# Queries and keys of the first two tiles of a banded attention made one stage earlier, part of the band mask moved from TensorE to VectorE, and fewer split steps on GpSimd

## The reference, cut to what matters

```python
# 1: linear attention with decay, 16 query heads, 4 key/value heads of 128, chunks of 64
x = layernorm(x + lightning(x, wq, wk, wv, wo))
# 2: attention over the channels: for each of 32 items the 256 channels are the
#    sequence, the 64 rows its features, 8 heads of width 8
q, k, v = split(x_item.T @ w_in.T + b_in)
scores = q k^T / sqrt(8)
scores = where(|i - j| <= 64, scores, finfo.min)      # the band
o = softmax(scores) @ v
y = relu(o @ w_out.T + b_out) * encodings
x = layernorm(x + y @ w_ct + b_ct)
```

## Time and profile before

| | |
|---|---|
| median of three runs | 3537.84 us (3532.89 to 3541.11) |
| the profiled execution | 3529.02 us |
| its span, first to last instruction | 3527.3 us |
| PE busy | 3259.2 us, 92% of the span |
| first stage | 0 to 379 us |
| banded stage | 379 to 691 us |
| granted clock of PE, mean | 0.965 |

### The profile page before, as it was taken

How to read it: one execution, slowest core, us unless ns; L and a number is a source line. 1 busy time by engine, 2 the same in 40 slices (tenths; PEclk the granted TensorE clock), 3 DMA queues, 4 the chain that set the end, 5 groups by cost and what they waited for, 6 DMA issues and landing times. The chain is left out here.

```text
span 3527.3 us, 95956 instructions
## 1 busy us (share of the span) xinstructions
PE 3259.2 (92%) x37316; PEld 2275.0 (64%) x37316; DVE 2351.7 (67%) x4366; ACT 1945.2 (55%) x5229; POOL 2083.7 (59%) x3086
## 2 busy tenths in 40 slices
PE   9999699897899999999999999999998688689996
PEld 6777466565577777777777777777776355356665
DVE  5555266534687888777787878788777588444443
ACT  1111155422576677666777677666775377545555
POOL 3333388643566666666666666666666267657774
PEclk9999699998999999999999999999999799899998
DMA  2000455100211111111111111111111456366655
GB/s 85 13 13 7 117 124 126 47 1 4 73 53 52 51 51 50 51 47 47 49 54 52 45 56 51 52 43 52 48 40 33 92 152 170 109 218 210 212 183 230
DMA packets 223129, 278.60 MB, mean 79 GB/s; under 512 B 58548, under 2 KB 186872, under 8 KB 216280
## 3 DMA queue, kind: packets, MB, share of 16 engines
q1 hardware_dynamic: 203340, 237.24, 23.6%
q0 software_dynamic: 18432, 34.96, 2.9%
q10 hardware_dynamic: 908, 0.27, 0.1%
HBM read 162.13 MB, written 125.83 MB: 82 GB/s over the span
## 5 line engine op out<-in xcount | busy, mean ns | idle before, releaser
L2215 PE MATMUL head_ring<-gd_xT,head_w 128*128 128x512 f32 x1024 | 507.8, 619 | 8.5 <-DMA head_w<-gd_w 5.4
L1547 POOL DMA_INDIRECT ytok<-exp_arena,exp_cur x256 | 251.1, 981 | 117.2 <-issue 72.1
L2543 DVE TENSOR_TENSOR head_Xs<-head_bx,head_join 128x512 bf16<-128x512 f32 x320 | 219.7, 686 | 81.7 <-PE head_bx L2257 81.7
L2215 PEld LDWEIGHTS head_ring<-gd_xT,head_w 128*128 128x128 f32 x1024 | 175.2, 191 | 147.4 <-issue 134.8
L2508 DVE SCALAR_TENSOR_TENSOR head_cb_V<-head_ring,head_taps,head_cb_V 128x504 f32<-128x504 f32 (+2 forms) x384 | 263.0, 726 | 2.8 <-ACT head_cb_V L2370 2.8
L2340 PE MATMUL head_by<-head_wo,head_ogT 128*128 128x256 f32 x1016 | 253.1, 392 | 7.1 <-ACT head_ogT L2450 0.4
L2224 PE MATMUL head_ring<-head_w,gd_xT 128*128 128x256 f32 x1024 | 257.4, 394 | 0.0
L2340 PEld LDWEIGHTS head_by<-head_wo,head_ogT 128*128 128x128 f32 x1016 | 182.5, 189 | 37.2 <-DVE rows_xc L2576 13.7
L2224 PEld LDWEIGHTS head_ring<-head_w,gd_xT 128*128 128x128 f32 x1024 | 185.3, 191 | 32.2 <-issue 0.3
L2415 ACT CAST head_Tt<-head_btt 128x512 bf16<-128x512 f32 x320 | 194.1, 607 | 17.8 <-PE head_btt L2265 16.0
L2435 ACT COPY head_U<-head_bu 128x512 f32<-128x512 f32 x256 | 137.4, 589 | 109.9 <-PE head_bu L2303 109.9
(11 more groups left out here) (366 smaller groups left out, 9293.1 us busy)
## 6 DMA issues: line engine op xcount, KB each, us to landing
xbuf<-head_blank SPq DMA_DIRECT2D x64, 552.0 KB
exp_arena<-xbuf SPq DMA_DIRECT2D x64, 552.0 KB, 5.3
head_gi<-scan SPq DMA_DIRECT2D x64, 256.0 KB, 4.8
ytok<-head_blank SPq DMA_DIRECT2D x64, 256.0 KB
exp_arena<-ytok SPq DMA_DIRECT2D x14, 1024.0 KB, 12.3
moe_w<-moe_w SPq DMA_DIRECT2D x32, 384.0 KB, 3.2
cb_Q<-qd SPq DMA_DIRECT2D x45, 192.0 KB
cb_K<-kd SPq DMA_DIRECT2D x45, 192.0 KB
```

Of the source, the lines that this page charges most:

```text
L1547: pool.indirect_dma_start(ytok, bass.IndirectOffsetOnAxis(ap=cur[i % AHEAD][s][:, b:b + 1], axis=0), y[i % RESULTS][s][:, b, :], None, bou ...
L2215: last = pe.matmul(b[:, :], w[:, c, FEAT[what]], xT[:, c, n % UNITS * N:n % UNITS * N + N], start=c == 0, stop=c == DC - 1)
L2543: dve.tensor_tensor((Ti if a == 0 else Xs)[:, :, :], bx[:, :].rearrange("p (q i) -> p q i", i=SEQ), join[:, a, :].unsqueeze(1).broadcast_t ...
```

## The change

Three things are done.

1. Tiles 0 and 1 of the banded stage are prepared in the last turn of the first stage. Behind slot 0's last output product PE makes q and k of both tiles from the rows that were stored in turn 0 and are loaded back (`first`). ACT adds the biases and makes the first bf16 parts, POOL the others in three steps, SP writes them to `qd` and `kd` and reads them back into their places. A class `Hold` keeps what outlives a stage: four places for Q and K of two tiles (they are where the first stage's weights `wqk` and its rotation tables were, and later hold `gi` and `ex` of the delta stage and Q and K of the second channel attention), the band, the identity and the query and key weights. A table `OPENING` says where the first occurrence of a step stands. The remaining weights are issued by ACT.
2. In the pairs 1, 4 and 6 of each eight (`SUMMED`) PE leaves the band matmul out, and DVE adds the band and takes the maximum with `tensor_tensor_reduce`, four times 192 elements. It writes the sums back to PSUM, where nobody reads them.
3. The first bf16 part is cast by ACT (a step "cast"), and the last rest is written as bf16 directly: three split steps on POOL in place of five, and four in place of five for the maxima. "turn" and "place" come one unit later, "ratio" one unit earlier.

```diff
+class Hold:
+    PLACE = 2 * D * 4
+    AHEAD = 2
...
@@ stage_lightning
+                store(TURNS - 1, 0)
+                for t in range(Hold.AHEAD):
+                    for i in range(3):
+                        if i:
+                            sp.wait_ge(split_step, t * 3 + i + 1)
+                        else:
+                            sp.wait_ge(cast_ready, t + 1)
+                        for half, scratch, copies in ((0, qd, (i,)), (1, kd, (i, i + 3) if i < 2 else (i,))):
+                            for row in copies:
+                                sp.dma_start(scratch[t, row * 8:row * 8 + 8, :].rearrange("d (j c) -> j d c", c=D),
+                                             part[t][:, i, half, :]).then_inc(spread_in[t], 16)
...
+                for t in range(Hold.AHEAD):
+                    sp.wait_ge(spread_in[t], 8 * 16)
+                    for i in range(3):
+                        rows = slice(i * 24, i * 24 + 24)
+                        sp.dma_start(hold.heads(2 * t)[rows, :, :].rearrange("p j c -> p (j c)"), qd[t, 0:24, :]).then_inc(gather_in, 16)
+                        sp.dma_start(hold.heads(2 * t + 1)[rows, :, :].rearrange("p j c -> p (j c)"), kd[t, i * 8:i * 8 + 24, :]).then_inc(gather_in, 16)
+                store(TURNS - 1, 1)
...
+                        if (turn, k, u) == (TURNS - 1, Y0, 0):
+                            pe.wait_ge(first_in, 5 * 16)
+                            for t in range(Hold.AHEAD):
+                                pe.matmul(bank_of[t][:, 0:D], xwq[:, :], first[:, t, :], start=True, stop=True)
+                                pe.matmul(bank_of[t][:, D:2 * D], xwk[:, :], first[:, t, :], start=True, stop=True).then_inc(twin_filled, 1)
...
@@ stage_banded
-    SLOTS, RING, GROUP, LAG, FIRSTS, BEHIND = 4, 12, 4, 32, 4, 6
+    SLOTS, RING, GROUP, LAG, BEHIND, AHEAD = 4, 12, 4, 32, 6, Hold.AHEAD
+    SUMMED = (1, 4, 6)
...
-    plan = {"prepare": -36, "split0": -35, "split1": -33, "split2": -31, "split3": -29, "split4": -27, "spread": -28, "gather": -17, "values": -2, "fetch": -8, "tops": 17, "turn": 21,
-            "place": 22, "unload": 53, "sort": 55, "invert": 56, "ratio": 58, "wo": 63, "ct": 66, "close": 67, "store": 70}
+    plan = {"prepare": -36, "cast": -35, "split0": -34, "split1": -32, "split2": -30, "spread": -28, "gather": -17, "values": -2, "fetch": -8, "tops": 17,
+            "turn": 22, "place": 23, "unload": 53, "sort": 55, "invert": 56, "ratio": 57, "wo": 63, "ct": 66, "close": 67, "store": 70}
+
+    OPENING = {"fetch": (0, -1), "prepare": (2, 8), "cast": (2, 9), "values": (0, 10), "split0": (2, 9), "split1": (2, 11), "split2": (2, 13),
+               "spread": (2, 14), "gather": (2, 19)}
...
-                        pe.matmul(b[:, 0:QB * KW], ident16[:, :], band16[:, :], start=True, stop=False, skip_group_check=True)
+                        plain = n % H // 2 in SUMMED
+                        if not plain:
+                            pe.matmul(b[:, 0:QB * KW], ident16[:, :], band16[:, :], start=True, stop=False, skip_group_check=True)
...
+                    elif what == "cast":
+                        act.wait_ge(qk_ready, n - AHEAD + 1)
+                        if n >= AHEAD + 2:
+                            act.wait_ge(spread_in[n % 2], (n - 2) // 2 * WRITES)
+                        act.copy(part[n % 2][:, 0, :, :], qk[n % 2][:, :, :]).then_inc(cast_ready, 1)
...
+                        if j // 2 in SUMMED:
+                            for a in range(2):
+                                for i in range(QB):
+                                    held = near[n // 2 % 2][:, a * 512 + i * KW:a * 512 + i * KW + KW]
+                                    last = dve.tensor_tensor_reduce(out=held, in0=held, in1=band[:, i * KW:i * KW + KW], scale=-1.0, scalar=3e38,
+                                                                    op0=ALU.add, op1=ALU.min, accum_out=top[t % 2][:, i, j + a:j + a + 1])
+                            last.then_inc(top_ready, 1)
+                        else:
...
-                        if step % 2 == 0:
-                            pool.tensor_copy(part[u][:, i, :, :], left[:, :, :]).then_inc(split_step, 1)
-                        else:
-                            pool.tensor_tensor(rest[u][:, :, :], left[:, :, :], part[u][:, i, :, :], ALU.subtract).then_inc(split_step, 1)
+                            pool.wait_ge(cast_ready, n - AHEAD + 1)
+                            pool.tensor_tensor(rest[u][:, :, :], qk[u][:, :, :], part[u][:, 0, :, :], ALU.subtract).then_inc(split_step, 1)
+                        elif step == 1:
+                            pool.tensor_copy(part[u][:, 1, :, :], rest[u][:, :, :]).then_inc(split_step, 1)
+                        else:
+                            pool.tensor_tensor(part[u][:, 2, :, :], rest[u][:, :, :], part[u][:, 1, :, :], ALU.subtract).then_inc(split_step, 1)
```

More of the change, by code:

```diff
@@ L133, in stage_lightning @@
         qk = [m.sb(f"qk{u}", [P, QK, N]) for u in U]
-        ra = [[m.sb(f"ra{u}{k}", [P, 512]) for k in range(2)] for u in U]
-        rb = [[m.sb(f"rb{u}{k}", [P, 512]) for k in range(2)] for u in U]
+        ra = [[late[:, 2 + k, :] for k in range(2)], [m.sb(f"ra1{k}", [P, 512]) for k in range(2)]]
+        rb = [[late[:, 4 + k, :] for k in range(2)], [m.sb(f"rb1{k}", [P, 512]) for k in range(2)]]
         v = [m.sb(f"v{u}", [P, TS, HKV * DH]) for u in U]
@@ L145, in stage_lightning @@
         bank = [[m.ps(f"bank{u}{k}") for k in range(4)] for u in U]
+        bank_of = [bank[0][(Y0 + 1 + t) % 4] for t in range(Hold.AHEAD)]
+        xwq, xwk, xbq, xbk, xbqs = hold.wq, hold.wk, hold.bq, hold.bk, hold.bqs
+        first = m.sb("first", [P, Hold.AHEAD, D])
+        twin = [qk[0][:, 2 * t:2 * t + 2, :] for t in range(Hold.AHEAD)]
+        part = [sT[0][:, t, 0:3 * D].bitcast(BF16).rearrange("p (c a k) -> p c a k", c=3, a=2) for t in range(Hold.AHEAD)]
+        SCALE = float(np.float32(1.0) / np.sqrt(np.float32(8)))
         BLOCK = 4
@@ L303, in _ @@
                                      b[:, :].rearrange("p (h n) -> p h n", h=2 * G)).then_inc(o_ready[u], 1)
+                        elif (turn, k, u) == (TURNS - 1, Y0, 0):
+                            act.wait_ge(first_in, 5 * 16)
+                            act.activation(xbqs[:, :], xbq[:, :], ACT.Copy, scale=SCALE).then_inc(scaled, 1)
+                            act.wait_ge(scaled, 1)
+                            for t in range(Hold.AHEAD):
+                                act.wait_ge(twin_filled, t + 1)
+                                act.activation(twin[t][:, 0, :], bank_of[t][:, 0:D], ACT.Identity, bias=xbqs[:, :], scale=SCALE)
+                                act.activation(twin[t][:, 1, :], bank_of[t][:, D:2 * D], ACT.Identity, bias=xbk[:, :]).then_inc(twin_ready, 1)
+                                act.wait_ge(twin_ready, t + 1)
+                                act.copy(part[t][:, 0, :, :], twin[t]).then_inc(cast_ready, 1)
             @block.vector
@@ L408, in timeline @@
             for what, offset in plan.items():
-                if (g - offset) % H == 0 and 0 <= (g - offset) // H < TILES:
-                    yield what, (g - offset) // H
+                n, shifted = (g - offset) // H, OPENING.get(what, (0, offset))
+                if (g - offset) % H == 0 and shifted[0] + (what in OPENING) <= n < TILES:
+                    yield what, n
+                if what in OPENING and g == shifted[1]:
+                    yield what, shifted[0]
     def since(n):
@@ L532, in _ @@
                             pe.wait_ge(*held)
-                        pe.matmul(misc[:, 0:T], w["xa_wq"][:, :], x[:, n, :], start=True, stop=True)
-                        pe.matmul(misc[:, T:2 * T], w["xa_wk"][:, :], x[:, n, :], start=True, stop=True).then_inc(qk_filled, 1)
-                        held = (qk_ready, since(n + 1))
+                        pe.matmul(misc[:, 0:T], hold.wq[:, :], x[:, n, :], start=True, stop=True)
+                        pe.matmul(misc[:, T:2 * T], hold.wk[:, :], x[:, n, :], start=True, stop=True).then_inc(qk_filled, 1)
+                        held = (qk_ready, n - AHEAD + 1)
                     elif what == "values":
@@ L626, in _ @@
             def _(act):
-                act.wait_ge(early_in, 16 * len(early))
-                act.activation(bq[:, :], bias["xa_bq"][:, :], ACT.Copy, scale=SCALE).then_inc(bq_ready, 1)
-                act.wait_ge(bq_ready, 1)
+                for t, name in loads:
+                    act.dma_start(t, A[name]).then_inc(weights_in, 16)
                 for what, n in timeline():
@@ L663, in _ @@
             def _(dve):
-                dve.wait_ge(weights_in, 16 * len(loads))
                 for what, n in timeline():
@@ L1274, in early_weights @@
                 lower(sp, i)
-        stage_cross(nc, xc, qd, kd, rows, xbuf, early_weights, A)
+        stage_cross(nc, xc, hold, qd, kd, rows, xbuf, early_weights, A)
         with ExitStack() as ctx:
```

203 lines of the change are left out of this document (111 added, 92 removed).

## The result

| | before | changed |
|---|---|---|
| median of the runs, us | 3535.4 (6 runs, 3532.89 to 3541.11) | 3510.19 (6 runs, 3504.28 to 3511.75) |
| profiled execution, its own time, us | 3529.02 | 3511.75 |
| its span, us; granted TensorE clock | 3527.3; 0.965 | 3510.0; 0.966 |

The ratio of the medians is 0.9929, 95% interval 0.9916 to 0.9942: faster by 25 us. The forecast was 3517.0 us, 20.8 less than the 3537.84 known then, with a range from 3503 to 3533. The table's "before" joins the three runs shown earlier with three made beside the changed kernel.

The account below looks back on a forecast made before the run. PE was taken to bound the kernel, busy 3259.2 of 3527.3 us, with POOL close behind in the banded tile. Start -23.9 and 14 steady tiles +3.1 gave -20.8 us, from 3537.84 to 3517.0 us; range 3503 to 3533.

Parts of the forecast that it names:

- C0: First output score of the banded stage, behind 32 units of near scores; forecast at 407.9 us instead of 431.8.
- the start: Opening of the banded stage: queries and keys of tiles 0 and 1 made earlier bring the first output score 23.9 us forward.
- 1.8 us on PE, which bounds that stage: First stage's last turn: four added f32 matmuls of 256 columns, 0.44 us each, lengthen it by 1.8 us.
- 8 us of cover: First stage's end: last read goes out at about 370, the store is due at 378.0, leaving 8 us.
- start gives less: Rival: late reads or a late tile 2 put the first output score at some 415, total 3524 us; 9%.
- The add-and-reduce: DVE's new instruction in summed pairs: 0.39 us each, between 0.33 and 0.55; a pair 1.56 us, +0.62.
- Prepare's wait: Unit 12 of a tile: PE waits 0.76 us for the misc bank, because ratio stands behind summed pair 4.
- Sort's wait: Turn one unit later, directly ahead of sort: PE waits 0.45 us a tile for ACT's copy of turn's result.
- GpSimd: 0 taken: Lighter POOL in the steady tile: at most 0.45 us a tile; nothing counted, 6 us kept for the range.
- The sum of a tile: Steady tile: -0.99 for the band matmuls, +0.76 and +0.45 for waits, +0.22 us; 14 tiles +3.1.
- the waits stay out: Rival: add-and-reduce costs 0.33 us, POOL's relief is felt, PE keeps nearly all 13.9 us; total 3500 us; 13%.
- DVE becomes the bound: Rival: add-and-reduce at half rate, 0.7 us each, a tile +2.5 us, 14 tiles +34, total 3548 us; 8%.

Follow-up runs that it names:

- e9: Changed kernel with the twelve reads of tiles 0 and 1 issued at the banded stage's start, not the first stage's end; 0.9915 of before, one run.
- e4: Changed kernel with summed pairs 1, 5 and 6 in place of 1, 4 and 6; 0.9941 of before, 15.95 us a tile.
- e8: Changed kernel with summed pairs 1, 5, 6 and turn and place back one unit earlier, at 21 and 22; 0.9968 of before, one run; 15.94 us a tile.
- e3: Changed kernel, mix kept, with GpSimd's old five split steps and five for the maxima, no cast on ACT; 0.9934 of before, 16.64 us a tile.
- e11: Changed kernel with summed pairs 1, 5, 6 and the third split step three units later (-27 for -30); 0.9917 of before, 15.45 us a tile.
- e2: Changed kernel with no summed pairs, all band matmuls back on PE, opening and lighter GpSimd kept; 0.9938 of before, 16.11 us a tile.
- e5: Changed kernel with the first stage's last store issued from ScalarE's queue; 0.9994 of before, one run; 16.35 us a tile.
- e10: The changed kernel itself, measured again beside a candidate; 0.9944 of before, 16.36 us a tile.
- e12: Changed kernel with summed pairs 1, 5, 6, third split three units later, turn and place back at 21 and 22; 0.9915 of before, 15.39 us a tile.
- e6: Changed kernel whose first stage's end doesn't wait for the twelve reads; PE waits for them in the banded stage; 0.9958 of before, one run.
- e7: Changed kernel with last store from ACT, reads not awaited, tile 0's reads behind the first third of tile 1's writes; 0.9975 of before, one run.

## Why the prediction was right, and where its steps were not

The time came out right and the shape too: a first near score that waits for no transfer of its own, C0 some 21 us earlier, a steady tile that gains nothing. In the banded stage's end the sum even falls on the microsecond (-20.76 against -20.8). That is luck in part, since terms were wrong in both directions: the start gave 2.7 us less than forecast, 14 tiles at -0.02 in place of +0.22 us gave 3.4 more, and 0.7 us stand in neither.

- **"1.8 us on PE, which bounds that stage": 0 in the two profiled executions.** The four pairs of records take 1.7 us (349.48 to about 351.2), but the last output product ends at 372.58, before at 372.69. PE stood idle 1.78 us before, waiting for DVE's la_sT, and after 0.84 there and 0.29 for la_oT. That covers 0.65 us. The rest is the clock (third number from the end): the 24 matmul records behind that wait took 4.5 us before, at 0.62, and 3.1 after, at 1.00. First before, then after:

```profile
354.13:358.61 4.48, 4.48 (x24) 3.38 (x25) 0.00 (x0) 2.13 (x4) 0.00 (x0) 0.62 0.10 34
```

```profile
349.00:358.50 9.50, 8.37 (x59) 5.63 (x58) 4.44 (x12) 5.94 (x12) 6.93 (x10) 1.00 0.22 62
```

If the clock had stayed up there before, part of the 1.8 us would presumably show; no other execution of before was profiled.

- **"8 us of cover": none.** I reckoned when the last read is issued (370, measured 370.99 with its own 0.36) and forgot what it carries. The step that failed is the store's cover, counted in issue time on the queue instead of in bytes: 2.36 MB were under way until 382, and the restart came 4.8 us late (7.4 against 2.6 in e9). This is the "start gives less" rival in its first half, at a smaller price; with the 1.8 us that weren't lost, the first near score came 2.5 us late (383.55 for 381.0) and C0 2.7 (410.59 for 407.9). From the one to the other it was 27.0 us, forecast 26.9: following SP's queue gave that. Inside, tile 2's prepare came 0.7 us later than taken, its first write 1.0 us sooner behind it, and C0 0.5 us later behind the place; the spreads, the landing and the reads took what was taken for them. (The sum in the prediction has a slip of 0.2 us: 381.0 + 4.4 is 385.4.)
- **The add-and-reduce: 0.39 us taken, 0.31 measured, below the lower bound of 0.33.** I had held that "nothing in the rows lets it cost less", with at least 0.06 for the read. A read is recorded with 0.14 us but starts together with the next main instruction and has no step of its own. The main instruction's 0.4 us record, too, overlaps the next by 0.08. A pair takes 1.20 to 1.24 us; by the drain rule of the Trainium skill (VectorE: DVE Perf Modes, The DRAIN you can't avoid) alone the prediction's estimate was 2.2, and the trace doesn't bear that out here.
- **Prepare's wait: 0.76 taken, 0.45 measured** (4.5 us in ten waits). The place and the instruction are the ones named. With pair 4 at 1.20 instead of 1.56 us the same working gives 0.33 + 0.17 - 0.10 = 0.40, so nearly the whole miss is the term above. e4 took the wait down to 0.20.
- **Sort's wait: 0.45 taken, 0.10 measured**, and e8 shows that it was worth nothing in the tile.
- **GpSimd: 0 taken; -0.29 us a tile shown by e3.** I kept it for the range. But PE's wait for the banding *grew*, from 3.9 to 6.4 us in nine tiles, because the cheaper and earlier PE arrives at V sooner and the third split stands in the way (e11 moves it and the wait goes). So relief and new wait are in one row, and only e3, with 9.1, takes them apart.
- **The sum of a tile:** -0.99 + 0.45 + 0.10 + 0.28 (V) = -0.16, measured -0.02, forecast +0.22. The terms that the waits show leave 0.14 us unexplained, and in e4 they promise 0.6 where 0.4 came. I haven't settled it. (The tile of before is 16.37 us, not 16.40: the 605.8 of the earlier trace rows is the second record of a prepare that starts at 605.50.)

The rival "the waits stay out" was false for the changed table and nearly true for e11's, whose tile is 0.9 us shorter than before: 12.9 us for 14 tiles, near the 13.9 that the mix could give. But 0.26 us of each tile are GpSimd's (16.37 to 16.11, e2); 0.66 us a tile, 9.2 us, lie between e2 and e11. "DVE becomes the bound" fell with the first pair: a step of 0.31 us where it decides from 0.6, and DVE is busy 61.4 of 80 us. The Trainium skill (Vector Engine (DVE) Microarchitecture Reference, Points that are easy to get wrong) gives a half rate for an S2S2D2_STT instruction with two non-bf16 sources in SBUF. The trace calls this one CUSTOM_DVE_ANT_0 and doesn't say whether it is of that shape. With one of its two sources in PSUM no half rate shows: at half rate, twice the 1.02 ns an element of the earlier trace rows, 192 elements alone would take 0.39 us, and the step is 0.31.

The medians differ by 25.2 us, the stage by 20.8 in the profiled executions. The difference isn't in any row: the profiled execution of before was 6.4 us under its median, that of after 1.6 above. The clock, below, can move a single execution by nearly as much. Of the signs that I had named as mine of being wrong none came (a tile of 17.5 us, 10 us of waiting for cb_top, the store behind 379), but of those of being right the first near score (380 to 382) and the step of the add-and-reduce (0.35 to 0.45) missed.

## What to carry to other kernels

Moving reads to the end of an earlier stage hides their latency, not their bytes (4.8 us here): count the bytes that are in flight when the stage's last store is issued, since a barrier waits for both. An operation moved from a bound engine to one with room pays only where the bound engine doesn't wait in order for what stands behind it; the same edit cost 0.24 us a tile in one slot and, one pair and one split later, gave 0.66 beside e2, whose split stood where the change puts it. Two edits made at once can cancel to no change: undo each before both are called useless.

## What the chip showed that I had not expected

Behind C0 the granted TensorE clock drops to 1.2 GHz in some executions and stays at 2.4 GHz in others. Busy times by stretch of the changed kernel, then of e5, which differs from it by one store's queue:

```profile
411.00:426.00 15.00, 15.00 (x94) 10.58 (x96) 7.46 (x25) 7.77 (x18) 6.56 (x13) 0.50 0.57 134
```

```profile
411.00:426.00 15.00, 14.54 (x157) 10.31 (x157) 11.37 (x40) 11.11 (x25) 12.57 (x27) 1.00 0.72 168
```

At half the clock 94 matmul records stand in 15 us, at the full one 157. From C0 to the next stage it is 259.5 us (260.1 in e10) against 254.5 in e5, which has the same tile: the fall costs 5 us; between e4 and e8 (255.6 and 249.5, again one tile) it is 6. What stood before it is a wait of PE for transfers, just ahead of its densest stretch. PE's waits in the last us before C0, of the changed kernel, of e12 (which fell) and of e5 (which didn't):

```profile
408.60 0.34 PE L646 MATMUL cb_near<-hold_band,hold_ident 128*128 128x384 bf16 x1 [0.57 <-DMA cb_K<-kd]
```

```profile
414.00 0.33 PE L671 MATMUL cb_score<-hold_place 75*128 75x192 bf16 x2 [1.97 <-DMA hold_place<-cb_topT]
```

```profile
411.27 0.33 PE L672 MATMUL cb_score<-hold_place 75*128 75x192 bf16 x2 [0.53 <-DMA hold_place<-cb_topT]
```

The changed kernel waited 0.57 us there and then the 1.49 at C0 shown with the result. Over all thirteen executions with the new start and the one of before, the six in which the clock fell at or behind C0 (changed, e4, e10, e11, e12, before) waited 1.4 to 3.1 us for transfers in the last 3 us before it, the others at most 0.6, save e8: 1.42 us and no fall, where e10 waited 1.37 and fell. So some 2 us of waiting go with 5 more behind them, and the line between is thin. It isn't shown that the wait is the cause. In e3, e6 and e7 the clock had fallen already, more than 12 us earlier; of e3:

```profile
399.00:408.00 9.00, 8.17 (x39) 4.95 (x38) 7.18 (x21) 0.37 (x1) 3.32 (x8) 0.50 0.81 166
```

There PE came to C0 0.6 to 1.8 us later than in the changed kernel and had no transfer to wait for. Counted from the first near score to the next stage, e6 and e7 take 283.8 and 283.7 us, e5 281.8, the changed kernel 286.5: they had paid a part ahead of C0. Of the executions with the new start only the changed kernel's, e4's and e10's show no low clock between 396 and 408. e12 was to settle whether the earlier turn keeps the clock up. It doesn't: where it expected a clock near 1.00, from 411 to 426, the clock was 0.65, and at C0 itself e12 waited longest of all, 1.97 us. No run took the wait away by itself.
